# Attention on one core: blocks of three half steps (four heads by 256 queries) with signals of their own, loop written out

## The chip, the cores and the metric

The kernel runs on one core of one Trainium2 chip. The metric is the device time of one execution in microseconds (us); shorter is better.

## The reference, cut to what matters

```python
x = L0_attn_x                                  # (4, 2048, 256)
xn = layernorm(x)
xh, xsh = xn[:, :, :128], holt(xn)[:, :, :128] # holt: exponential smoothing over the sequence
# two branches, each: 8 heads of 16
scores = einsum('bshd,bthd->bhst', q, k) / 4
a = softmax(scores); o = einsum('bhst,bthd->bshd', a, v)
x1 = layernorm(xh + o1 @ wo1.T + bo1); x2 = layernorm(xsh + o2 @ wo2.T + bo2)
y = concatenate([x1, x2], -1)
y = layernorm(y + relu(y @ w_ff1.T + b_ff1) @ w_ff2.T + b_ff2)
out = x + y + (relu(xn @ W1 + b1) @ W2 + b2)   # the "second net"
```

What the change touches is the attention: for each of 4 batches, 2 branches and 8 heads, 2048 by 2048 scores, their exponential, and the product with the values.

## The kernel before, in words

Five engines run programs of their own, tied by semaphores. Each batch has a prologue (normalise, transpose, projections, smoothing, a bound on the maximum), the attention, and the nets that finish the batch. `batches` (L232) runs the prologue of batch 0, then a hardware loop (`Fori`) of three rounds over `middle` (attention of b, prologue of b + 1, nets of b), then `last` written out. Inside the loop, values that a wait compares with depend on b and are computed in registers; in `last` they are constants.

The attention of a batch is 16 units (2 branches, 2 groups of four heads, 4 chunks of 512 queries). A unit runs over 16 key tiles (kt) of 128 keys, so 32 half steps (`STEPS`), and before the change a half step is two heads by 512 queries. On TensorE (PE), in program order (`attention`, L1142):

- scores (L1157): four matmuls per kt, 50 rows by 128 columns, 512 columns moving. The two heads of a half step use the two halves of the array's rows and run side by side. A half step fills one of three PSUM slots of 1024 columns; it waits for the exponential three half steps before.
- one part of the second net (`second_hidden` or `second_out_part`, L994 through `narrow`): 24 matmuls of 256 columns in four column groups, at the eight kts of `NET_KTS` (`FIRST_NET_KTS` in the first unit of a batch); the output projection of the unit before at kt 8, 32 records in the trace.
- values (L1183): four matmuls per kt in four column groups, f32, two records each in the trace, added up in `o_bank`. They wait for both exponentials of the kt and, at kt 0, until DVE has read `o_bank` (`evict`, L679).

The order is scores of kt + 1, then the net's part or the projection, then values of kt. Each of these groups is named S, N or V below. ScalarE (ACT, L585) takes each slot through the exponential into one of four buffers of `p_sb`. DVE evicts and divides a unit's result, takes the bias and relu of the net's hidden part (`hidden_half`, L722), and is still finishing the previous batch (`finish`, L746 to L769) when an attention starts. `second_hidden` waits, from its second part on, until DVE has read the part before (`hid2_read`). POOL and SP issue the DMAs; POOL also adds biases and refills `k_st` and `q_st` when a group's values are done.

## Time and profile before

| | |
|---|---|
| median of 3 runs | 2676.5 us (2676.16 to 2676.57) |
| the profiled execution | 2678.51 us, span 2677.0 us, mean granted clock 0.98 |
| PE busy | 94% of the span |
| ACT busy | 82% |
| DVE busy | 57% |
| POOL busy | 13% |

PE is TensorE's matmuls, PEld its weight loads, ACT ScalarE, DVE VectorE, POOL GpSimd. A row of the timeline merges equal instructions that follow without idle time; the end of a matmul is modelled, so the distance between starts says more than the length. In brackets stands the idle time before, and what ended it.

### The profile page before, as it was taken

How to read it: one execution, taken by the hardware profiler on the slowest of the kernel's cores; microseconds unless marked ns; L12 is line 12 of the kernel's file. 1: busy time of each engine (PE TensorE's matmuls, PEld its weight loads, DVE VectorE, ACT ScalarE, POOL GpSimd, SP SyncE). 2: the span in 40 equal slices, each digit the busy share in tenths (PEclk: the TensorE clock that was granted, in tenths of full speed). 3: DMA queues.
4: the chain of work that ended last, by engine and by line, in shares of the span. 5: the costliest groups of instructions: out<-in, count | busy, mean ns of one | idle time of the engine just before them, and what ended most of it. 6: DMA issues, size and time to landing. Idle time of an engine off the chain costs nothing.

```text
span 2677.0 us, 75084 instructions
## 1 busy us (share of the span) xinstructions
PE 2529.1 (94%) x30049; PEld 1004.4 (38%) x30049; DVE 1516.9 (57%) x3228; ACT 2190.8 (82%) x2411; POOL 355.2 (13%) x349
## 2 busy tenths in 40 slices
PE   5799999999999999998999999999999999999976
PEld 3233333335633333333663333333464333333344
DVE  5344555565764555556575455555567545555576
ACT  3699999994479999997449999999556999999933
POOL 0201010003410100000440101000144010100142
PEclk9899999999999999999999999999999999999988
DMA  4602010003120202000411102000041010100001
GB/s 159 122 10 34 10 34 10 10 10 104 50 65 10 34 14 38 10 6 12 115 49 57 30 14 34 10 10 6 21 122 48 10 34 10 34 10 10 6 25 45
DMA packets 50612, 96.38 MB, mean 36 GB/s; under 512 B 8768, under 2 KB 33344, under 8 KB 49872
## 3 DMA queue, kind: packets, MB, share of 16 engines
q1 hardware_dynamic: 41808, 71.99, 8.9%
q0 software_dynamic: 8448, 19.41, 4.4%
q8 instruction: 251, 4.11, 0.6%
q14 instruction: 105, 0.86, 0.1%
HBM read 57.23 MB, written 34.08 MB: 34 GB/s over the span
## 4 chain that ended last, share of the span: by engine, by line
PE 80%; DVE 7%; issue 5%; POOL 4%; ACT 1%; DMA 1%; SPq 0%; DVEq 0%; POOLq 0%; ACTq 0%
PE slot L1183 34%; PE slot L1157 20%; PE slot L994 16%; POOL p_sb L495 3%; PE slot L1227 2%; PE slot L1079 2%; PE slot L1215 2%; PE slot L1109 1%; DVE o_sb L679 1%; PE slot L1118 1%; PE slot L1107 1%; DVE hid_one L722 1%; DMA k_st<-part_dram 1%; PE slot L1060 1%; ACT p_sb L585 1%
## 5 line engine op out<-in xcount | busy, mean ns | idle before, releaser
L585 ACT ACTIVATE p_sb<-slot 128x1024 f32<-128x1024 f32 x2048 | 1915.7, 1029 | 125.1 <-PE slot L1157 122.4
L1183 PE MATMUL slot<-p_sb,v_sb 128*17 128x512 f32 x8192 | 1071.4, 597 | 23.2 <-DVE o_sb L679 12.6
L1157 PE MATMUL slot<-q_st,k_st 50*128 50x512 f16 x4096 | 624.5, 384 | 23.4 <-DMA k_st<-part_dram 15.4
L1157 PEld LDWEIGHTS slot<-q_st,k_st 50*128 50x128 f16 x4096 | 126.8, 94 | 896.4 <-ACT p_sb L585 715.8
L722 DVE TENSOR_SCALAR hid_one<-slot,b_grown 128x256 f32<-128x256 f32 x256 | 123.8, 484 | 298.9 <-PE slot L994 289.0
L1183 PEld LDWEIGHTS slot<-p_sb,v_sb 128*17 128x17 f32 x8192 | 180.2, 97 | 241.4 <-ACT p_sb L585 211.5
L734 DVE SCALAR_TENSOR_TENSOR second<-slot,second 128x256 f32<-128x256 f32 x64 | 27.2, 425 | 371.1 <-PE slot L994 371.1
L688 DVE RECIPROCAL rden<-den 128x256 f32<-128x256 f32 x128 | 224.4, 1753 | 7.5
L994 PE MATMUL slot<-xt_parts,w_parts 128*32 128x256 f16 x6144 | 214.8, 274 | 1.6 <-DVE hid_one L722 1.6
L994 PE MATMUL slot<-w_parts,hid_parts 128*32 128x256 f16 x6144 | 214.7, 274 | 0.0
L1227 PE MATMUL slot<-wf_parts,p_sb 128*128 128x256 f16 x1536 | 178.0, 275 | 8.7 <-POOL p_sb L495 8.6
L1215 PE MATMUL slot<-area,wf_parts 128*128 128x512 f16 x768 | 173.0, 385 | 12.0 <-DVE area L749 7.2
L994 PEld LDWEIGHTS slot<-xt_parts,w_parts 128*32 128x32 f16 x6144 | 141.0, 96 | 107.7 <-issue 103.0
L994 PEld LDWEIGHTS slot<-w_parts,hid_parts 128*32 128x32 f16 x6144 | 141.2, 96 | 106.6 <-issue 104.6
L486 POOL TENSOR_TENSOR resid<-resid,con 128x1024 f32<-128x1024 f32 x16 | 37.7, 2356 | 1053.7 <-DVEq L744 1053.7
L495 POOL TENSOR_TENSOR p_sb<-area,p_sb 128x512 f16<-128x512 f32 x128 | 148.0, 1157 | 135.7 <-ACT p_sb L601 125.9
L1227 PEld LDWEIGHTS slot<-wf_parts,p_sb 128*128 128x128 f16 x1536 | 149.7, 99 | 36.1 <-POOL p_sb L495 14.7
L368 POOL DMA_DIRECT2D k_st<-part_dram x48 | 24.2, 511 | 954.4 <-PE slot L1183 954.2
L716 DVE TENSOR_TENSOR resid<-slot,resid 128x512 f32<-128x512 f32 x64 | 44.2, 691 | 181.9 <-PE slot L994 181.9
L600 ACT ACTIVATE area<-slot,bf_grown 128x512 f32<-128x512 f32 x128 | 88.0, 687 | 66.2 <-PE slot L1215 39.9
L726 DVE TENSOR_TENSOR hid_parts<-hid_one,hid_parts 128x256 f16<-128x256 f32 x256 | 109.0, 426 | 9.1 <-DVE hid_parts L724 0.5
L1215 PEld LDWEIGHTS slot<-area,wf_parts 128*128 128x128 f16 x768 | 74.8, 99 | 103.9 <-issue 11.2
(101 smaller groups left out, 1833.0 us busy)
## 6 DMA issues: line engine op xcount, KB each, us to landing
part_dram<-p_sb SPq DMA_DIRECT2D x16, 1024.0 KB, 4.0
q_st<-part_dram POOLq DMA_DIRECT2D x96, 128.0 KB, 7.9
xn<-x SPq DMA_DIRECT2D x16, 512.0 KB, 7.6
second<-x SPq DMA_DIRECT2D x32, 256.0 KB, 3.9
ffn_dram<-second SPq DMA_DIRECT2D x32, 256.0 KB, 2.0
area<-ffn_dram SPq DMA_DIRECT2D x16, 512.0 KB, 4.8
out<-area SPq DMA_DIRECT2D x16, 512.0 KB, 3.2
k_st<-part_dram SPq DMA_DIRECT2D x48, 128.0 KB, 12.3
```

What stands on the lines that cost most here:

```text
L495: pool.tensor_tensor(h_lo[:, m, :], h_one[:, m % 2, :], h_hi[:, m, :], ALU.subtract).then_inc(hid_ready, 1)
L585: act.activation(p_sb[:, n % 4, :], slot[n % 3][:, :], ACT.Exp, scale=0.25 / GROW ** 2).then_inc(exp_done, 1)
L600: act.activation(h_one[:, m % 2, :], bank, ACT.Relu, bias=bf_grown[:, m:m + 1])
L688: step(dve.reciprocal(rden[:, cols], den[:, cols]))
L722: dve.tensor_scalar(hid_one[:, :], bank, b1_grown[:, k:k + 1], 0.0, ALU.add, ALU.max).then_inc(hid2_read, 1)
L726: dve.tensor_tensor(hid_lo[:, k, :], hid_one[:, :], hid_hi[:, k, :], ALU.subtract).then_inc(hid2_ready, 1)
L994: mm = pe.matmul(out[ROW * r:ROW * (r + 1), :], lhs[:, ROW * r:ROW * (r + 1)], rhs, start=start, stop=stop, skip_group_check=True)
L1079: mm = pe.matmul(slot[(first + i) % 4][:, k * CHUNK:(k + 1) * CHUNK], wqk[:, 2 * a + which, :], xt[a][:, (2 * i + k) * CHUNK:(2 * i + k + ...
L1157: mm = pe.matmul(slot[at % 3][:, k * CHUNK:(k + 1) * CHUNK], k_st[rows_, pair, kt * P:(kt + 1) * P], q_st[rows_, pair, c_ * CHUNK:(c_ + 1) ...
L1183: mm = pe.matmul(o_bank[ROW * j:ROW * j + DK + 1, :], v_sb[:, a, kt, GH * g + j, :], p_sb[:, n % 4, (j % 2) * CHUNK:(j % 2 + 1) * CHUNK], ...
L1215: mm = pe.matmul(slot[m // 2 % 2][:, (m % 2) * CHUNK:(m % 2 + 1) * CHUNK], w[:, k, m * P:(m + 1) * P], src[:, k * CHUNK:(k + 1) * CHUNK], ...
L1227: mm = pe.matmul(bank[:, t * D:(t + 1) * D], src[:, m, t * P:(t + 1) * P], w[:, m, :], start=(m == 0 and r == 0), stop=(m == HB - 1 and r ...
```

## The change

A half step becomes four heads by 256 queries of one kt (an even half step takes the first half of the chunk, an odd one the second). The 32 half steps of a unit are put into blocks of three (ten of three and one of two). On PE the order is: the scores of a block, each half step into its own of three slots; then the values of the previous block; then a part of the second net or the projection. Each half step has its own exponential, its own signal of scores, of exponential and of values. `p` has six buffers, the third of each block lying in `area`. All hardware loops over batches become Python loops, on all engines. PSUM is one tensor, cut into slots.

```diff
+BLOCKS = [(3 * i, min(3 * i + 3, STEPS)) for i in range(-(-STEPS // 3))]
+LAST_BLOCK = len(BLOCKS) - 1
+HALF_CHUNK = CHUNK // 2
-NET_KTS, FIRST_NET_KTS, PROJECTION_KT = [0, 2, 4, 6, 10, 12, 14, 15], [6, 8, 10, 11, 12, 13, 14, 15], 8
+NET_BLOCKS, FIRST_NET_BLOCKS, PROJECTION_BLOCK = [0, 1, 3, 4, 6, 8, 9, 10], [3, 4, 5, 6, 7, 8, 9, 10], 5
...
+        def batches_in_line(eng, prologue, middle, last):
+
+            prologue(0)
+            for b in range(B - 1):
+                middle(b)
+            last(B - 1)
...
+            p_flat = p_sb[:, :, :].rearrange("p i n -> p (i n)")
+            p_first = p_flat[:, 0:2 * SLOT], p_flat[:, 2 * SLOT:4 * SLOT]
+            p_third = area[:, 3 * SLOT:4 * SLOT], area[:, 0:SLOT]
...
-                    for n in range(UNITS2 * STEPS):
-                        act.wait_ge(scores_made, UNITS2 * STEPS * b + n + 1)
-                        if n % 2 == 0:
-
-                            act.wait_ge(pv_done, UNITS2 * TILES * b + n // 2 + 1)
-                        act.activation(p_sb[:, n % 4, :], slot[n % 3][:, :], ACT.Exp, scale=0.25 / GROW ** 2).then_inc(exp_done, 1)
+                    for unit in range(UNITS2):
+                        u = UNITS2 * b + unit
+                        for i, (lo, hi) in enumerate(BLOCKS):
+                            block = len(BLOCKS) * unit + i
+                            for n in range(lo, hi):
+                                act.wait_ge(scores_made, STEPS * u + n + 1)
+                                if n == lo and block >= 2:
+
+                                    done = BLOCKS[i - 2][1] + (0 if i >= 2 else -STEPS)
+                                    act.wait_ge(pv_done, STEPS * u + done)
+                                p = p_third[block % 2] if n == lo + 2 else p_first[block % 2][:, (n - lo) * SLOT:(n - lo + 1) * SLOT]
+                                act.activation(p, slot[n - lo][:, :], ACT.Exp, scale=0.25 / GROW ** 2).then_inc(exp_done, 1)
...
-                    flat = area[:, 0:2 * FF]
+                    dve.wait_ge(stored, 16 * (CHUNKS * (B - 1) + 1))
+                    flat = area[:, SLOT:SLOT + 2 * FF]
...
-                with step.over(B - 1, PER_MIDDLE) as b:
+                for b in range(B - 1):
                     middle(b)
...
+                        lo, hi = BLOCKS[i]
+                        for n in range(lo, hi):
+
+                            before = n - 3 if i > 0 else (n - 2 if n < 2 else n - 5)
+                            if STEPS * u + before >= 0:
+                                pe.wait_ge(exp_done, STEPS * u + before + 1)
+                            if n == 2 and unit == 0:
                                 pe.wait_ge(ff_read, CHUNKS * b + 1)
+                            kt, tok = n // 2, c_ * CHUNK + n % 2 * HALF_CHUNK
+                            for j in range(GH):
+                                pair, rows_ = GH // 2 * g + j // 2, slice(HALF * (j % 2), HALF * (j % 2) + ROWS)
+                                at = SLOT * (n - lo) + CHUNK * (j % 2) + HALF_CHUNK * (j // 2)
+                                mm = pe.matmul(banks[:, at:at + HALF_CHUNK], k_st[rows_, pair, kt * P:(kt + 1) * P],
+                                               q_st[rows_, pair, tok:tok + HALF_CHUNK], start=True, stop=True)
                             mm.then_inc(scores_made, 1)
...
+                        if i == 0:
+
+                            pe.wait_ge(o_read, u + 1)
+                            if unit == 0:
+                                pe.wait_ge(ff_read, CHUNKS * b + 2)
+                        for n in range(lo, hi):
+                            pe.wait_ge(exp_done, STEPS * u + n + 1)
+                            kt, cols = n // 2, slice(n % 2 * HALF_CHUNK, (n % 2 + 1) * HALF_CHUNK)
+                            p = (p_first if n < lo + 2 else p_third)[block % 2]
+                            for j in range(GH):
+                                at = SLOT * ((n - lo) % 2) + CHUNK * (j % 2) + HALF_CHUNK * (j // 2)
+                                mm = pe.matmul(o_bank[ROW * j:ROW * j + DK + 1, cols], v_sb[:, a, kt, GH * g + j, :], p[:, at:at + HALF_CHUNK],
+                                               start=(n == 0), stop=(n >= STEPS - 2), skip_group_check=True)
+                            mm.then_inc(pv_done, 1)
+
+                    for unit in range(UNITS2):
+                        net_blocks = FIRST_NET_BLOCKS if unit == 0 else NET_BLOCKS
+                        for i in range(len(BLOCKS)):
+
+                            scores(unit, i)
+                            if i > 0:
+                                values(unit, i - 1)
+                            elif unit > 0:
+                                values(unit - 1, LAST_BLOCK)
+                            if i in net_blocks:
+                                (second_out_part if unit % 2 else second_hidden)(b, unit // 2, net_blocks.index(i))
+                            if i == PROJECTION_BLOCK and unit > 0:
                                 out_projection(b, unit - 1)
+                    values(UNITS2 - 1, LAST_BLOCK)
```

## Rows read from the trace of the kernel before

**Rows 1.** The page's chain that ended last: shares by engine, and by line.
```profile
PE 80%; DVE 7%; issue 5%; POOL 4%; ACT 1%; DMA 1%; SPq 0%; DVEq 0%; POOLq 0%; ACTq 0%
PE slot L1183 34%; PE slot L1157 20%; PE slot L994 16%; POOL p_sb L495 3%; PE slot L1227 2%; PE slot L1079 2%; PE slot L1215 2%; PE slot L1109 1%; DVE o_sb L679 1%; PE slot L1118 1%; PE slot L1107 1%; DVE hid_one L722 1%; DMA k_st<-part_dram 1%; PE slot L1060 1%; ACT p_sb L585 1%
```

**Rows 2.** Windows, exponentials (L585) alone, four stretches: us, ACT busy (count), PEclk.
```profile
95.90:594.80 498.90, 479.39 (x512) 0.99 0.11 23
750.50:1248.40 497.90, 479.31 (x512) 0.99 0.10 22
...
2049.70:2543.20 493.50, 477.59 (x512) 1.00 0.08 17
sum 1988.60, ACT 1915.71; mean ACT 478.93
```

**Rows 3.** Timeline, PE, last batch: start, us, engine, line, operation, out<-in, count.
```profile
2176.42 0.60 PE L1157 MATMUL slot<-q_st,k_st 50*128 50x512 f16 x4
2176.95 0.84 PE L994 MATMUL slot<-xt_parts,w_parts 128*32 128x256 f16 x24
2177.62 1.03 PE L1183 MATMUL slot<-p_sb,v_sb 128*17 128x512 f32 x8
2178.59 0.61 PE L1157 MATMUL slot<-q_st,k_st 50*128 50x512 f16 x4
2179.12 1.05 PE L1183 MATMUL slot<-p_sb,v_sb 128*17 128x512 f32 x8
2180.11 0.61 PE L1157 MATMUL slot<-q_st,k_st 50*128 50x512 f16 x4
```

**Rows 4.** Timeline, PE, last batch: a projection and the values behind it.
```profile
2191.77 1.08 PE L994 MATMUL slot<-con,att 128*32 128x128 f32 x32
2192.67 1.04 PE L1183 MATMUL slot<-p_sb,v_sb 128*17 128x512 f32 x8
```

**Rows 5.** Timeline, ACT, last batch, over a unit.
```profile
2163.59 13.03 ACT L585 ACTIVATE p_sb<-slot 128x1024 f32<-128x1024 f32 x14 [0.19 <-PE slot L1157]
...
2179.02 14.87 ACT L585 ACTIVATE p_sb<-slot 128x1024 f32<-128x1024 f32 x16 [0.23 <-PE slot L1157]
2194.07 2.85 ACT L585 ACTIVATE p_sb<-slot 128x1024 f32<-128x1024 f32 x3 [0.19 <-PE slot L1157]
```

**Rows 6.** Timeline, last batch, unit boundary: the eviction on DVE, and values on PE.
```profile
2146.33 0.74 DVE L679 STREAM_SHUFFLE o_sb<-slot 128x512 f32<-128x512 f32 x1
...
2147.12 1.05 PE L1183 MATMUL slot<-p_sb,v_sb 128*17 128x512 f32 x8 [0.24 <-DVE o_sb L679]
```

**Rows 7.** Timeline, first batch (in the loop): scores, and the exponential that waits for them.
```profile
257.63 0.60 PE L1157 MATMUL slot<-q_st,k_st 50*128 50x512 f16 x4
258.14 1.02 ACT L585 ACTIVATE p_sb<-slot 128x1024 f32<-128x1024 f32 x1 [0.53 <-PE slot L1157]
```

**Rows 8.** The chain that ended last, in order of time: start, us, what.
```profile
738.38 8.36 PE slot L1227 x75
```

**Rows 9.** Timeline, PE, end of batch 0's attention: values, then a net's part.
```profile
593.14 1.03 PE L1183 MATMUL slot<-p_sb,v_sb 128*17 128x512 f32 x8
594.00 0.83 PE L994 MATMUL slot<-w_parts,hid_parts 128*32 128x256 f16 x24
```

**Rows 10.** Timeline, last batch, first unit: DVE, PE, and the next unit's start on ACT.
```profile
2054.06 6.78 DVE L635 TENSOR_SCALAR rs<-mv 128x4 f32<-128x4 f32 x1
...
2067.18 0.48 DVE L722 TENSOR_SCALAR hid_one<-slot,b_grown 128x256 f32<-128x256 f32 x1 [0.21 <-DVE area L768]
...
2067.72 0.84 PE L994 MATMUL slot<-xt_parts,w_parts 128*32 128x256 f16 x24 [1.55 <-DVE hid_one L722]
...
2082.12 1.94 ACT L585 ACTIVATE p_sb<-slot 128x1024 f32<-128x1024 f32 x2 [0.23 <-PE slot L1157]
```

**Rows 11.** Timeline, PE: first scores behind a loop's end, and behind the last round.
```profile
749.86 0.23 PEld L1157 LDWEIGHTS slot<-q_st,k_st 50*128 50x128 f16 x4 [3.40 <-issue]
...
2049.30 0.82 PE L1157 MATMUL slot<-q_st,k_st 50*128 50x512 f16 x6
```

More of the change, by code:

```diff
@@ L212, in rows @@
             return con[:, lo:hi].rearrange("p (k n) -> p k n", k=1).broadcast_to([P, k, hi - lo])
-        slot = [ctx.enter_context(nc.psum_tensor(f"slot{i}", [P, SLOT], f32)) for i in range(4)]
+        banks = ctx.enter_context(nc.psum_tensor("banks", [P, 4 * SLOT], f32))
+        slot = [banks[:, i * SLOT:(i + 1) * SLOT] for i in range(4)]
         def sem(name):
@@ L434, in last @@
                     attention(b, False)
-                    hold(sp, pv_done, TILES * UNITS2 * (b + 1) + 2)
+                    hold(sp, pv_done, STEPS * UNITS2 * (b + 1))
                     results(b)
@@ L449, in sync_program @@
                         sp.dma_start(k_st[at:at + 2, pair, :], k_ones).then_inc(ones_out, 16)
-                batches(sp, prologue, middle, last)
+                batches_in_line(sp, prologue, middle, last)
                 sp.wait_ge(second_out, 16 * (HALVES * B + 2))
@@ L527, in pool_program @@
                 pool.wait_ge(ones_out, 16 * HEADS)
-                batches(pool, first, middle, last)
+                batches_in_line(pool, first, middle, last)
             def scalar_program(act):
@@ L625, in scalar_program @@
                 act.wait_ge(consts_in, 16)
-                batches(act, first, middle, last)
+                batches_in_line(act, first, middle, last)
             def vector_program(dve):
@@ L677, in evict @@
                     u = UNITS2 * b + n
-                    hold(dve, pv_done, TILES * (u + 1) + 2)
+                    hold(dve, pv_done, STEPS * (u + 1))
                     dve.stream_shuffle(o_sb[:, :], o_bank, O_ROWS).then_inc(o_read, 1)
@@ L793, in turn @@
                         src = slot[place % 4][:, 0:P]
-                        if a == 1 or not isinstance(b, int):
+                        if 2 * b + a > 0:
                             dve.wait_ge(m_out, 16 * (2 * b + a))
@@ L1142, in attention, with scores @@
                 def attention(b):
-                    def scores(unit, kt):
+                    def scores(unit, i):
                         a, g, c_ = UNIT_LIST[unit]
-                        if kt == 0 and c_ == 0:
+                        u = UNITS2 * b + unit
+                        if i == 0 and c_ == 0:
                             hold(pe, stack_in[g], 16 * ((K_LOADS + 2 * Q_LOADS) * b + (Q_LOADS, K_LOADS + 2 * Q_LOADS)[a]))
@@ L1148, in scores @@
                                 hold(pe, k_first_in[g], 16 * K_LOADS * (b + 1))
-                        for n in (2 * kt, 2 * kt + 1):
-                            at = STEPS * unit + n
-                            pe.wait_ge(exp_done, UNITS2 * STEPS * b + at - 2 + 3)
-                            if at == 2:
-                                pe.wait_ge(ff_read, CHUNKS * b + 1)
-                            for k in range(2):
-                                pair, rows_ = GH // 2 * g + n % 2, slice(HALF * k, HALF * k + ROWS)
-                                mm = pe.matmul(slot[at % 3][:, k * CHUNK:(k + 1) * CHUNK], k_st[rows_, pair, kt * P:(kt + 1) * P],
-                                               q_st[rows_, pair, c_ * CHUNK:(c_ + 1) * CHUNK], start=True, stop=True)
+                        lo, hi = BLOCKS[i]
@@ L1159, in scores, with values @@
                             mm.then_inc(scores_made, 1)
-                    scores(0, 0)
-                    for unit, (a, g, c_) in enumerate(UNIT_LIST):
+                    def values(unit, i):
+                        a, g, c_ = UNIT_LIST[unit]
                         u = UNITS2 * b + unit
-                        net_kts = FIRST_NET_KTS if unit == 0 else NET_KTS
-                        for kt in range(TILES):
-                            if kt + 1 < TILES:
-                                scores(unit, kt + 1)
-                            elif unit + 1 < UNITS2:
-                                scores(unit + 1, 0)
-                            if kt in net_kts:
-                                (second_out_part if unit % 2 else second_hidden)(b, unit // 2, net_kts.index(kt))
-                            if kt == PROJECTION_KT and unit > 0:
-                                out_projection(b, unit - 1)
-                            if kt == 0:
-                                pe.wait_ge(o_read, u + 1)
-                                if unit == 0:
-                                    pe.wait_ge(ff_read, CHUNKS * b + 2)
-                            pe.wait_ge(exp_done, STEPS * u + 2 * kt + 2 + 3)
-                            for j in range(GH):
-                                n = 2 * kt + j // 2
-                                mm = pe.matmul(o_bank[ROW * j:ROW * j + DK + 1, :], v_sb[:, a, kt, GH * g + j, :],
-                                               p_sb[:, n % 4, (j % 2) * CHUNK:(j % 2 + 1) * CHUNK],
-                                               start=(kt == 0), stop=(kt == TILES - 1), skip_group_check=True)
-                            mm.then_inc(pv_done, 1)
@@ new lines, in values @@
+                        lo, hi = BLOCKS[i]
+                        block = len(BLOCKS) * unit + i
+                        if i == 0:
[11 more added lines that the diff above has]
+                            mm.then_inc(pv_done, 1)
@@ L1250, in last @@
                     nets(b)
-                pe.sem_inc(pv_done, 2)
                 pe.sem_inc(net_done, 1)
                 pe.wait_ge(consts_in, 16)
-                batches(pe, first, middle, last)
+                batches_in_line(pe, first, middle, last)
                 pe.wait_ge(added, 2)
```

4 lines of the change are left out of this document (1 added, 3 removed).

## The prediction

> **What bounds the kernel now.** I read the page first: the chain that ended last is 80% PE, and over half of it is two lines, values (L1183) and scores (L1157) [rows 1]. The windows on L585 come next: the 2048 exponentials fill four stretches, 1988.6 us of the 2677.0 us, one per batch with 16 units each [rows 2]. So a unit is about 31 us, and there are 64.
>
> The order of time on PE shows what a unit is made of [rows 3]. I call S the scores of one kt, V its values, N one part of the second net. S to the next group takes 0.53 us, N 0.67, V up to the following S 0.99 after an S and 0.97 after an N. A kt without N is 1.52 us, one with N 2.17. Sixteen kts, eight Ns and one projection of 0.90 [rows 4] make 16 x 1.52 + 8 x 0.65 + 0.90 = 30.4 us on PE. ACT needs 2.85 us for three exponentials [rows 5] and 1.02 for one [rows 7], so 0.917 each in a stream, 29.3 us a unit. A unit of the last batch lasts 30.48 us (2163.59 to 2194.07 [rows 5]), the mean of a batch inside the loop is 497.9 / 16, about 31.0 [rows 2]. So **PE's in-order stream is the bound, and ACT is only 1.1 us a unit behind it**. What exceeds 30.4 is, in every second unit, V waiting for the DVE eviction at a boundary (0.24 us of PE idle, some 0.4 in all [rows 6]); and, inside the loop, ACT starting 0.51 us after its scores (257.63 to 258.14 [rows 7]) where the written-out last batch has 0.43 (2178.59 to 2179.02 [rows 3, 5]).
>
> **The change, part by part.**
>
> *Cost of the pieces.* Scores: before, two rounds of 512 columns take 0.53 with about 0.10 of changeover, 0.215 a round. After, a half step is two rounds of 256 columns, each with its own weights. Lower bound 0.215; upper from the second linear layer of the net, 75 matmuls of 256 columns with their own weights in 8.36 us [rows 8], 0.111 a round, 0.223. I take 0.220. Values: V takes about 0.86 of its 0.99, so half the columns take 0.431. The leading 0.014 after an S stays. Changeovers: S to V or N 0.10, V to S 0.11. V to N costs nothing: 593.14 to 594.00 is 0.86 for a whole V [rows 9]. **N to S does not occur in the trace** (N is always followed by V today), and the change makes it the rule, 8 times a unit. Bounds: 0, as N to V, and 0.11, as V to S. I take 0.11, since N like V is a four-column-group form and S a two-row-group form, and each change between these two kinds that the trace shows costs 0.10 or 0.11.
> The Trainium skill ("TensorEngine Tiling (Array Packing)", Key Properties) says that a change of tiling mode, not merely of tile, drains the engine. The trace agrees for S to V and V to S, and by that rule N to S is a drain too.
>
> *A block on PE.* Three score half steps 0.66 + 0.11, three value half steps 1.31, N 0.655, changeover 0.11: 2.84 us. ACT's three exponentials: 2.75. Without N a block is 2.18, with the projection 3.08. PE saves five pairs of changeovers a unit (11 instead of 16, about 1.1 us), adds a little for more rounds, and would need about 29 us, under ACT's 29.3. If the two overlapped freely this would be a gain of 1 to 1.5 us a unit.
>
> *The new wait.* They don't overlap freely. Slot 2 is freed by the last exponential of the previous block, and the third S of a block waits for it. Behind that wait in PE's queue stand all values of the previous block, N or the projection, and the first scores of the next block; ACT has then just three exponentials left. From the end of that exponential to the end of the first of the block after: signal about 0.05 (my estimate, no row times it alone), S 0.22 + 0.10, V 1.31, N 0.655, changeover 0.11, scores to exponential 0.43 [rows 3, 5], exponential 1.02 [rows 7]: 3.90 us. ACT could have been there after 4 x 0.917 = 3.67. So **a block with N that follows a loose one stalls ACT 0.23**; one that follows a tight block stalls by PE's own excess, 0.09; the projection block 0.33. The short block is the worst: between the scores of block 10 and those of the next unit stand two S, three V and N, 2 x 0.22 + 0.11 + 1.31 + 0.655 + 0.11 = 2.62, and they are covered by two exponentials, 1.83: a stall of 0.79. Iteration 0 has only two V and is loose again. N stands in blocks 0, 1, 3, 4, 6, 8, 9, 10, the projection in 5: stalls after block 1, 3 and 8 of 0.23 each, 4, 6 and 9 of 0.09 each, 5 of 0.33, 10 of 0.79, in all 2.08. **A unit: 29.33 + 2.08 = 31.4 us**, against a mean of 31.0 (loop) or 30.7 (last batch) now. In this the boundary wait for DVE is gone: V of the next unit comes after N and three S, 1.5 us or more behind the last V, and the eviction takes 0.74 [rows 6].
>
> *First unit of batches 1 to 3.* N parts start at block 3, the second at block 4, about 13 us into the batch. But DVE is still finishing the previous batch, with one step of 6.78 us, and it reads the first part only at 2067.18, 17.9 us after the first scores (2049.30). Already now PE waits 1.55 us there, at kt 8, and the unit lasts 32.4 (first exponential 0.43 after 2049.30, next unit's 2082.12) [rows 10, 11]. After, it waits at block 4, with 12 value half steps done instead of 16. From 18.4 us: N and changeover 0.76, five blocks of 2.84, 2.62 for the last, so 36.0 us for the unit. Batch 0 has no such wait, yet its stretch is 1.0 us longer than that of batch 1 [rows 2]: some 2 us of slow start, which stay, on 31.0 for a first unit without the wait (eight blocks with N, no short block ahead), 32.9.
>
> *Sum of attention, first exponential's start to last one's end.* The last unit counts to its last end, 31.4 - 0.79 - 0.92 + 1.02 = 30.7. Batch 0: 32.9 + 14 x 31.4 + 30.7 = 503.2. Batches 1 to 3: 36.0 + 439.6 + 30.7 = 506.3 each. Together 2022.1 against 1988.6 [rows 2]: **+33.5 us**.
>
> *Loop written out.* After the last net matmul PE idles 3.40 us where the loop closes; after the last iteration the first scores follow at 2049.30 with no such idle [rows 11]. Two such places, about 3.2 each: -6.4. In the prologues inside the loop the waits lose their register work too. The trace has no row for one hop of them but ACT's, 0.51 against 0.43 [rows 3, 5, 7]; with some ten such hops in series that is about 1 us a prologue (0 to 2): -3. The nets stay: PE streams there. The shorter ACT delay (0.43) is in the units above.
>
> *End of attention.* The last V after the last exponential is one half step, 0.43, not a whole V, 0.86: about -0.5 x 4 = -2. SP, POOL: same DMAs, the same points of release (pv_done counts half steps; the last V of a unit still releases the stacks). The third buffer lies in memory that only prologue and results use; last batch's weight tests now wait for stores finished long before. Nothing for these.
>
> **Sum:** 33.5 - 6.4 - 3 - 2 = +22 us. The profiled execution took 2678.5 us with a span of 2677.0, 2 us over the median 2676.5, so I add the difference to the median: 2699, **+0.8%**.
>
> **The rivals.**
>
> *Faster: the changeover from N to S is hidden.* Then every net block loses 0.11, the stalls of 0.09 vanish, those of 0.23 become 0.12, the short block 0.68; a unit is about 30.75, and 60 ordinary units give 60 x 0.65 = 39 us back: 2660. The sign turns at a changeover of about 0.05. For it: N to V and V to N are free. Against: both keep the form of the groups, N to S doesn't. 0.17.
>
> *Scores of 256 columns do not pair.* If the second pair of a half step can't load its weights under the first, a round grows by a load, and at the worst the four matmuls of a half step run one by one: 4 x 0.107 = 0.43 instead of 0.22. PE would then bound every block, 0.64 more in each: some 5 us a unit, near 3000. Against: N's loads, same length, hide at 256 columns (24 matmuls in 0.67 us, four side by side [rows 3]).
> The Trainium skill ("TensorE: Matmul & The Clock Gate", The mechanism) says a weight load overlaps running matmuls only when the row group differs, which is this rival's result; N's rows speak against it, since all its groups use the same rows. 0.05.
>
> *PE's instruction supply.* A unit holds 1216 weight loads and matmuls instead of 832, 39 a us instead of 27. The densest long stretch now is a run of kts with N, 72 in 2.17 us, 33 a us; for 0.67 us N alone runs at 72. If 33 were a limit a unit would be 36.8, again near 3000. 0.03.
>
> *No change within 0.2%* (about what a measurement of this kernel can tell from none: 2671 to 2682): DVE's wait in the first units smaller, a changeover of 0.05 to 0.07. 0.09.
>
> *Forecast* 2682 to 2722: 0.66. Chances: faster 0.17, same 0.09, slower 0.74. The range reaches to the faster rival and, above, to rounds of 0.24 or values at 0.44 (0.2 to 0.3 a unit): 2657 to 2725.
>
> **What would show it.** A second unit in mid-batch of 31.4 us, ACT idle about 0.7 to 0.8 once a unit behind scores of the first block; idles near 0.2 after net blocks; N's last round to the next S about 0.2 us; no wait on DVE o_sb; a PE wait of some 5 us on hid_one in batches 1 to 3; PE's 3.4 us idle at the two loop ends gone; ACT 0.43 after its scores everywhere. Wrong if a unit is under 31.0 (then N to S or the short block is mis-sized) or over 32.

## The result and the profile after

The changed kernel took 2720.1 us (median of 4 runs, 2716.8 to 2721.8) against 2676.5: a ratio of 1.0161, interval 1.0143 to 1.0178. It is slower, by 43.6 us. The profiled execution took 2716.8 us, with a span of 2715.2. Every ratio below is to the kernel before, measured again beside each experiment (medians 2678.5, 2677.6 and 2677.5). Two single executions, one of the kernel before and one of halves_only, took 4160 and 4158 us at a mean granted clock of 0.56 and are left out of every comparison.

The page of after: the engines, the queue that brings instructions, and the chain that ended last, by engine and by line.

```profile
PE 2499.7 (92%) x42337; PEld 1486.3 (55%) x42337; DVE 1516.0 (56%) x3228; ACT 2202.2 (81%) x2411; POOL 353.9 (13%) x349
...
q8 instruction: 334, 5.47, 0.8%
...
PE 68%; ACT 20%; DVE 6%; issue 2%; DMA 2%; POOL 2%; SPq 0%; DVEq 0%; ACTq 0%; POOLq 0%
PE banks L1201 27%; PE banks L1181 14%; PE banks L1013 13%; ACT p_sb L604 12%; ACT area L604 6%; PE banks L1259 5%; PE banks L1247 4%; PE banks L1098 2%; PE banks L1128 1%; POOL p_sb L508 1%; DVE rs L653 1%; DMA part_dram<-p_sb 1%; PE banks L1126 1%; ACT p_sb L620 1%; ACT area L619 1%
```

ACT had 1% of the chain before [rows 1] and has 20% now: the chain passes from PE to ACT and back in every unit, which is what a handshake looks like that neither engine wins. PE is 29 us less busy than before (2499.7 against 2529.1) and the span is 38 us longer.

The exponentials' windows, answering to [rows 2]: us, ACT busy (count), PEclk, DMA share, GB/s.

```profile
95.83:600.03 504.20, 482.09 (x512) 0.99 0.10 23
749.54:1259.93 510.39, 482.01 (x512) 0.99 0.09 22
1408.74:1919.10 510.36, 482.01 (x512) 0.99 0.10 22
2067.70:2578.07 510.37, 482.01 (x512) 0.99 0.08 18
sum 2035.32, ACT 1928.12; mean ACT 482.03
```

Attention grew by 46.7 us (forecast 33.5). Between the stretches lie 446.9 us, against 458.7 in [rows 2]: 11.8 us less. After the last exponential come 137.1 us against 133.8. That adds up to the 38.2 us of the spans; the medians differ by 5 more, since before's profiled execution was 2.0 us above its median and after's 3.3 below. Single runs scatter by more than that: after's by 5 us, and before's, 30 single runs in all, from 2675.0 to 2686.5.

One ordinary unit of the last batch, ACT. The starts give the length of every block (the ends are modelled):

```profile
2135.28 1.94 ACT L604 ACTIVATE p_sb<-banks 128x1024 f32<-128x1024 f32 x2
2137.90 1.94 ACT L604 ACTIVATE p_sb<-banks 128x1024 f32<-128x1024 f32 x2 [0.68 <-PE banks L1181]
...
2140.63 1.96 ACT L604 ACTIVATE p_sb<-banks 128x1024 f32<-128x1024 f32 x2
...
2143.65 1.94 ACT L604 ACTIVATE p_sb<-banks 128x1024 f32<-128x1024 f32 x2
...
2152.23 1.94 ACT L604 ACTIVATE p_sb<-banks 128x1024 f32<-128x1024 f32 x2
...
2155.35 1.94 ACT L604 ACTIVATE p_sb<-banks 128x1024 f32<-128x1024 f32 x2 [0.27 <-PE banks L1181]
...
2169.39 1.94 ACT L604 ACTIVATE p_sb<-banks 128x1024 f32<-128x1024 f32 x2 [0.68 <-PE banks L1181]
```

A unit is 2169.39 - 2137.90 = 31.49 us; the forecast was 31.4. The two exponentials of the short block take 2137.90 - 2135.28 = 2.62 us instead of 1.83: a stall of 0.79, exactly the forecast one. Block 1 takes 3.02 (2140.63 to 2143.65), a stall of 0.27 over 2.75; forecast 0.23. Block 5, with the projection, takes 2155.35 - 2152.23 = 3.12, 0.37; forecast 0.33. All eleven blocks of this unit, from the starts of the same view, the left-out ones too: 2.73, 3.02, 2.72, 3.02, 2.84, 3.12, 2.84, 2.73, 3.01, 2.84, 2.62.

PE over blocks with a net part, the same unit:

```profile
2146.56 0.39 PE L1181 MATMUL banks<-q_st,k_st 50*128 50x256 f16 x4 [0.52 <-ACT area L604]
2146.88 1.06 PE L1201 MATMUL banks<-p_sb,v_sb 128*17 128x256 f32 x16
2147.75 0.61 PE L1201 MATMUL banks<-area,v_sb 128*17 128x256 f32 x8
2148.18 0.84 PE L1013 MATMUL banks<-xt_parts,w_parts 128*32 128x256 f16 x24
2148.96 0.83 PE L1181 MATMUL banks<-q_st,k_st 50*128 50x256 f16 x12
2149.72 1.06 PE L1201 MATMUL banks<-p_sb,v_sb 128*17 128x256 f32 x16
```

From values to values it is 2149.72 - 2146.88 = 2.84 us, the forecast block. Three scores with their changeover take 0.76 (forecast 3 x 0.22 + 0.10), two value half steps 0.87, the third 0.43. **N to S is 0.78, where N to V was 0.67 [rows 3]: the unknown changeover is 0.11.** The [0.52] ahead of the third scores is the wait for slot 2, the new wait.

### The profile page after: what moved, and what is told of

It reads as the page before. It is cut to its first block, busy times and chain, and to the rows that moved or that the text cites. A ratio compares the mean times of both kernels' runs of the same rounds, so it can differ in the third digit from the quotient of the medians.

```text
span 2715.2 us, 93007 instructions
## 1 busy us (share of the span) xinstructions
PE 2499.7 (92%) x42337; PEld 1486.3 (55%) x42337; DVE 1516.0 (56%) x3228; ACT 2202.2 (81%) x2411; POOL 353.9 (13%) x349
## 3 DMA queue, kind: packets, MB, share of 16 engines
q8 instruction: 334, 5.47, 0.8%
## 4 chain that ended last, share of the span: by engine, by line
PE 68%; ACT 20%; DVE 6%; issue 2%; DMA 2%; POOL 2%; SPq 0%; DVEq 0%; ACTq 0%; POOLq 0%
PE banks L1201 27%; PE banks L1181 14%; PE banks L1013 13%; ACT p_sb L604 12%; ACT area L604 6%; PE banks L1259 5%; PE banks L1247 4%; PE banks L1098 2%; PE banks L1128 1%; POOL p_sb L508 1%; DVE rs L653 1%; DMA part_dram<-p_sb 1%; PE banks L1126 1%; ACT p_sb L620 1%; ACT area L619 1%
## 5 line engine op out<-in xcount | busy, mean ns | idle before, releaser
L604 ACT ACTIVATE p_sb<-banks 128x1024 f32<-128x1024 f32 x1408 | 1369.3, 1029 | 152.7 <-PE banks L1181 126.8
L1201 PE MATMUL banks<-p_sb,v_sb 128*17 128x256 f32 x11264 | 751.1, 385 | 0.0
L1181 PE MATMUL banks<-q_st,k_st 50*128 50x256 f16 x8192 | 618.6, 273 | 103.0 <-ACT area L604 83.4
L604 ACT ACTIVATE area<-banks 128x1024 f32<-128x1024 f32 x640 | 668.0, 1044 | 0.0
L1181 PEld LDWEIGHTS banks<-q_st,k_st 50*128 50x128 f16 x8192 | 309.4, 94 | 392.6 <-issue 162.6
L1201 PEld LDWEIGHTS banks<-p_sb,v_sb 128*17 128x17 f32 x11264 | 260.0, 97 | 290.2 <-issue 137.7
L1201 PE MATMUL banks<-area,v_sb 128*17 128x256 f32 x5120 | 396.2, 382 | 0.0
L1013 PE MATMUL banks<-xt_parts,w_parts 128*32 128x256 f16 x6144 | 217.0, 275 | 11.4 <-DVE hid_one L740 11.4
L1013 PE MATMUL banks<-w_parts,hid_parts 128*32 128x256 f16 x6144 | 214.5, 273 | 0.0
L1259 PE MATMUL banks<-wf_parts,p_sb 128*128 128x256 f16 x1536 | 175.9, 273 | 7.9 <-POOL p_sb L508 7.9
L1259 PEld LDWEIGHTS banks<-wf_parts,p_sb 128*128 128x128 f16 x1536 | 149.0, 98 | 33.9 <-POOL p_sb L508 13.2
```

The costliest lines, as they stand in the source:

```text
L604: act.activation(p, slot[n - lo][:, :], ACT.Exp, scale=0.25 / GROW ** 2).then_inc(exp_done, 1)
L1013: mm = pe.matmul(out[ROW * r:ROW * (r + 1), :], lhs[:, ROW * r:ROW * (r + 1)], rhs, start=start, stop=stop, skip_group_check=True)
L1181: mm = pe.matmul(banks[:, at:at + HALF_CHUNK], k_st[rows_, pair, kt * P:(kt + 1) * P], q_st[rows_, pair, tok:tok + HALF_CHUNK], start=True ...
L1201: mm = pe.matmul(o_bank[ROW * j:ROW * j + DK + 1, cols], v_sb[:, a, kt, GH * g + j, :], p[:, at:at + HALF_CHUNK], start=(n == 0), stop=(n ...
L1259: mm = pe.matmul(bank[:, t * D:(t + 1) * D], src[:, m, t * P:(t + 1) * P], w[:, m, :], start=(m == 0 and r == 0), stop=(m == HB - 1 and r ...
```

## The experiments

### The loop alone

```diff
 # kernel before, all five programs and DVE's own loop
-                batches(pe, first, middle, last)
+                batches_in_line(pe, first, middle, last)
...
-                with step.over(B - 1, PER_MIDDLE) as b:
+                for b in range(B - 1):
                     middle(b)
```

> The kernel before with its hardware loops over batches written out and nothing else. My theory (the new blocks cost, the written-out loop gives back): a unit in batches 0 to 2 falls from a mean of 31.0 to the last batch's 30.7, 48 x 0.31 = 15 us, the two loop ends give 6.4, the prologues 3: 2652 us. Rival (writing the loop out is itself a cost, for instance by instruction supply): 2677 or more, units at 31.0 or above.

Measured, loop_only: 2656.8 us (2656.1 to 2660.6), ratio 0.9918, interval 0.9901 to 0.9935; forecast 2652. PE at the first loop end, and ACT in batch 0:

```profile
729.20 8.36 PE L1234 MATMUL slot<-wf_parts,p_sb 128*128 128x256 f16 x75 [0.32 <-POOL p_sb L502]
737.50 0.82 PE L1164 MATMUL slot<-q_st,k_st 50*128 50x512 f16 x6
```
```profile
209.17 13.04 ACT L592 ACTIVATE p_sb<-slot 128x1024 f32<-128x1024 f32 x14 [0.19 <-PE slot L1164]
...
224.60 14.87 ACT L592 ACTIVATE p_sb<-slot 128x1024 f32<-128x1024 f32 x16 [0.23 <-PE slot L1164]
239.65 13.04 ACT L592 ACTIVATE p_sb<-slot 128x1024 f32<-128x1024 f32 x14 [0.19 <-PE slot L1164]
...
255.52 14.87 ACT L592 ACTIVATE p_sb<-slot 128x1024 f32<-128x1024 f32 x16 [0.66 <-PE slot L1164]
```

The 3.40 us of [rows 11] are gone. Units alternate between 30.48 (209.17 to 239.65) and 30.92 (224.60 to 255.52), and all four stretches last 493.0 to 493.7 us, what only the written-out batch did before [rows 2]. So writing the loop out gains about 20 us by itself, 15 of it in attention, and the rest of the change costs more than the 43.6 us that were measured: about 63.

### Half steps of four heads by 256 queries, in the old order

```diff
 # loop_only, scores
-                            for k in range(2):
-                                pair, rows_ = GH // 2 * g + n % 2, slice(HALF * k, HALF * k + ROWS)
...
+                            for j in range(GH):
+                                pair, rows_ = GH // 2 * g + j // 2, slice(HALF * (j % 2), HALF * (j % 2) + ROWS)
+                                col = CHUNK * (j % 2) + CHUNK // 2 * (j // 2)
...
 # values: a half step at a time, each with its wait
+                            for n in (2 * kt, 2 * kt + 1):
+                                pe.wait_ge(exp_done, STEPS * u + n + 1 + 3)
```

> loop_only with the half step of four heads by 256 queries, each half step of the values waiting for its own exponential; the order per kt (scores of the next, net, values), the three slots and the four buffers stay as before, no blocks of three. My theory (it is the grouping in blocks of three that costs, not the smaller matmuls): within 0.4 us a unit of loop_only, so 2652 to 2672. Rival (256-column matmuls with twice the weight loads and signals cost the time): a unit of 31.5 or more, 2700 or above.

Measured, halves_only: 2664.8 us, ratio 0.9939, interval 0.9918 to 0.9960; 8 us more than loop_only. The units are 30.96 and 30.53, 0.04 above loop_only's. So 256 columns pair as well as 512, PE takes 39 instructions a us, and two of the rivals (some 3000 us) fall. Most of the rest, 6.8 us, is in one or two longer units of every batch, the fifth and the ninth, by up to 1.8 us, where POOL refills `k_st` and `q_st`. In the last batch PE stops some 12 us behind the start of the refill (2157.16). PE there, and the window around it (us, busy time of PE, PEld, DVE, ACT and POOL, PEclk, DMA share, GB/s):

```profile
2168.78 0.61 PE L1194 MATMUL slot<-p_sb,v_sb 128*17 128x256 f32 x8
2170.44 0.63 PE L1194 MATMUL slot<-p_sb,v_sb 128*17 128x256 f32 x8 [1.06 <-ACT p_sb L592]
```
```profile
2167.00:2171.00 4.00, 2.94 (x60) 1.33 (x53) 2.18 (x5) 3.25 (x4) 0.00 (x0) 1.00 1.03 131
```

ACT is named as the releaser, but ACT itself idles here (3.25 us busy in a window of 4.00), so the cause is another. The DMA engines are busy throughout this window (share 1.03), and in the trace the instruction queue's 16 KB packets, which came every 6 to 7 us up to here, come at 2156.16 and then only at 2167.13. That PE had run out of fetched code fits these rows and was not tested by itself.

### The net's last part moved from block 10 to block 7

```diff
-NET_BLOCKS, FIRST_NET_BLOCKS, PROJECTION_BLOCK = [0, 1, 3, 4, 6, 8, 9, 10],
+NET_BLOCKS, FIRST_NET_BLOCKS, PROJECTION_BLOCK = [0, 1, 3, 4, 6, 7, 8, 9],
```

> The changed kernel with one part of the second net moved from block 10, before the short cover of two exponentials, to block 7. My theory: at the unit's boundary PE then has 1.96 us between the last scores of a unit and the first of the next, and the stall there falls from 0.79 to about 0.13, with 0.06 more beside it; a unit of 30.85 instead of 31.49, 60 x 0.64 = 38 us off: 2682 us. Rival (the boundary stall comes from the eviction on DVE or from the signals there): the 0.79 stays, 2720.

Measured, net_10_to_7: 2685.7 us (10 runs, 2681.8 to 2686.3), ratio 1.0021, interval 1.0010 to 1.0032: 34 us less than after (forecast 38), for one net part moved. ACT over a unit:

```profile
2144.68 3.90 ACT L604 ACTIVATE p_sb<-banks 128x1024 f32<-128x1024 f32 x4
...
2175.58 3.90 ACT L604 ACTIVATE p_sb<-banks 128x1024 f32<-128x1024 f32 x4
```

A unit is 30.90 us (forecast 30.85), and the boundary has no idle time worth a bracket. The short block's stall is real: moving the part is worth 0.59 a unit. after's order put a net part behind the one block that has two exponentials to cover it.

### The net's part before the values

```diff
                             scores(unit, i)
+                            if i in net_blocks:
+                                (second_out_part if unit % 2 else second_hidden)(b, unit // 2, net_blocks.index(i))
...
                             if i > 0:
                                 values(unit, i - 1)
```

> The changed kernel with the net's part or the projection between the scores and the values instead of behind the values. The changeovers are as many, but it is V and not N that stands ahead of the scores. Theory (a changeover of 0.10 to 0.11 between four column groups and two row groups, the same for N and V; the path behind the third scores holds the same work): a unit of 31.4 to 31.6 again, 2720. Rival (the change from N to the scores is a cost of the new order): a unit of 30.8, 2680.

Measured, net_before_values: 2729.1 us, ratio 1.0193, interval 1.0176 to 1.0210. PE around a net part:

```profile
2157.04 0.84 PE L1013 MATMUL banks<-xt_parts,w_parts 128*32 128x256 f16 x24
2157.70 1.04 PE L1201 MATMUL banks<-p_sb,v_sb 128*17 128x256 f32 x16
2158.57 0.60 PE L1201 MATMUL banks<-area,v_sb 128*17 128x256 f32 x8
2159.10 0.92 PE L1181 MATMUL banks<-q_st,k_st 50*128 50x256 f16 x12
```

N takes 0.66 now, but the values' last piece takes 0.53 (2158.57 to 2159.10) instead of 0.43: the changeover has moved from N to V, at 0.10. Half of the units are 31.43 us, as forecast. The other half are 31.87: with the net one values' group earlier, its part also asks earlier for what DVE has read, which the waits show.

```profile
PE banks L1013 <- DVE hid_one L740: 26.2, 31, 5.3
```

In after it is 3 waits, 11.4 us. The price by the changeover is settled; that order is worse for a reason that was not in the expectation.

### Less of the net

```diff
                         for n, (src, w) in enumerate(((hid_hi, w2_hi), (hid_hi, w2_lo), (hid_lo, w2_hi))):
-                            mm = narrow(side[:, t * D:(t + 1) * D], src[:, m, t * P:(t + 1) * P], w[:, m, :], ...
 # and so in the hidden part
```

> The changed kernel with the second net's parts cut from six rounds of matmuls to one (two terms of three, and most of the sum, are left out, so its output is not the reference's); all signals stay. Theory (the stalls come from PE work behind the third scores of a block): ACT streams, with one stall of some 0.4 at the projection, a unit of 29.8, near 2620. Rival (the waits and signals of each half step, or six buffers, stall ACT by themselves): stalls of 0.2 stay in many blocks, a unit above 30.5.

Measured, thin_net: 2609.2 us, in a single run. ACT over a unit:

```profile
2129.92 1.94 ACT L604 ACTIVATE p_sb<-banks 128x1024 f32<-128x1024 f32 x2 [0.36 <-PE banks L1182]
...
2159.72 1.94 ACT L604 ACTIVATE p_sb<-banks 128x1024 f32<-128x1024 f32 x2 [0.36 <-PE banks L1182]
```

A unit is 29.80, as forecast: 32 exponentials at 0.917 are 29.34, and the one stall that is left belongs to the projection's block. With little net behind the slot's wait the structure does reach ACT's rate. So it is not the waits and signals as such that cost. This kernel also has less work on PE in all, so alone it doesn't separate how much PE does from where it stands. net_10_to_7 does: the same work, one part elsewhere in the queue, 0.59 us a unit. The total is 11 us under the forecast since the first units of batches 1 to 3 also shrank, to 35.0 to 35.6.

### POOL's addition later

The 9.94 us addition of a bias on POOL (L485) runs while DVE finishes the previous batch. This kernel holds it back until the last row block of `finish` is through. In after, last batch, the two stand like this:

```profile
2072.47 6.79 DVE L653 TENSOR_SCALAR rs<-mv 128x4 f32<-128x4 f32 x1
```
```profile
2069.28 9.94 POOL L485 TENSOR_TENSOR resid<-xn,con 128x4096 f32<-128x4096 f32 x1 [10.37 <-DVE area L776]
```

```diff
                     pool.wait_ge(ff_read, CHUNKS * b + 2)
+                    pool.wait_ge(o_ready, CHUNKS * b + 1)
                     pool.tensor_tensor(resid[:, :, :], xn[:, :, :], rows("bo", TILES), ALU.add).then_inc(xn_used, 1)
```

> The changed kernel, POOL's 9.94 us residual addition of the next batch held back until DVE has finished the previous batch. Theory: DVE's step of over 6 us in the first unit is a wait for POOL's operation; without it DVE reads the first net part some 6.6 us sooner, PE waits no longer at block 4, the clock stays at 1.0 there, and the first unit of batches 1 to 3 falls from 38.7 to 31.5 to 32.5: 19 to 21 us off, 2700 us. Rival (the step is long by itself): 2720, unchanged. If only the wait goes and the low clock stays, the first unit is about 34.

Measured, pool_late: 2720.7 us, ratio 1.0153, interval 1.0136 to 1.0170: no change against after. The forecast gain of some 20 us did not come, and DVE, POOL and PE tell why.

```profile
2081.32 7.23 DVE L743 CAST hid_parts<-hid_one 128x256 f16<-128x256 f32 x1
```
```profile
2079.49 8.91 POOL L486 TENSOR_TENSOR resid<-xn,con 128x4096 f32<-128x4096 f32 x1 [19.64 <-DVE area L787]
```
```profile
2089.70 1.47 PE L1014 MATMUL banks<-xt_parts,w_parts 128*32 128x256 f16 x24 [3.92 <-DVE hid_one L741]
```

The step of 6.8 us in `finish` is gone, but a cast that takes 0.29 elsewhere takes 7.23 now, and both end where POOL's addition ends (in after 2079.26 and 2079.22, here 2088.55 and 2088.40). PE waits 3.92 us one block later. **The long DVE step was never DVE's: it is one DVE instruction held until POOL's long one is over**, and moving POOL's moved the victim. POOL's own took 8.91 us here and 9.94 in after, where a DVE addition with two inputs in SBUF had started just ahead of it.

The Trainium skill ("SBUF — State Buffer", Who interferes with whom) has this rule: the two engines share a pair of ports as a lock for a whole instruction, which on DVE's side a cast or a tensor-scalar can want, and the one that comes second waits. Trace and rule agree, and I had read the 6.78 us of [rows 10] as given, where the rule would have led to POOL.

### POOL's addition in eight pieces

```diff
-                    pool.tensor_tensor(resid[:, :, :], xn[:, :, :], rows("bo", TILES), ALU.add).then_inc(xn_used, 1)
+                    for k in range(HB):
+                        pool.wait_ge(hid2_ready, HB * HALVES * b + k + 1)
+                        part = slice(2 * k, 2 * k + 2)
+                        pool.tensor_tensor(resid[:, part, :], xn[:, part, :], rows("bo", 2), ALU.add).then_inc(resid_part, 1)
```

> The changed kernel with POOL's residual addition cut into eight pieces of two tiles, each released when DVE has finished one part of the first unit's hidden layer, when DVE waits for PE anyway. Theory (POOL's long operation holds DVE wherever it stands, the wait then stops PE for 4 us and the granted clock falls to 0.5 behind it): no PE wait on hid_one over 0.5 us, clock 1.0 from 2080 on, the first unit of batches 1 to 3 is 32 to 33 instead of 38.7, 2700 us. Rival (the first unit is long by its blocks of nets alone): 37 or more, 2715.

Measured, pool_spread: 2698.7 us (2698.2 to 2705.2), ratio 1.0077, interval 1.0060 to 1.0094: 21 us less than after. POOL and the same DVE step, last batch, and the first unit's two ends on ACT:

```profile
2076.53 1.28 POOL L489 TENSOR_TENSOR resid<-xn,con 128x512 f32<-128x512 f32 x1 [21.20 <-DVE hid_parts L750]
```
```profile
2068.44 0.17 DVE L659 TENSOR_SCALAR rs<-mv 128x4 f32<-128x4 f32 x1
```
```profile
2064.11 1.94 ACT L610 ACTIVATE p_sb<-banks 128x1024 f32<-128x1024 f32 x2 [10.02 <-PE banks L1187]
...
2095.21 1.94 ACT L610 ACTIVATE p_sb<-banks 128x1024 f32<-128x1024 f32 x2 [0.68 <-PE banks L1187]
```

0.17 us where it was 6.79, and a first unit of 31.10 instead of 38.71. Batches 1 to 3 have 32.0, 31.1 and 31.1: 7.3 us less each on average, 22 in all, which fits the 21 us between the medians. (32.0 is the one of the three in which the clock fell just behind the start of the batch.)

The profiled execution itself shows only 11.5 of them (span 2703.7 against 2715.2). It was 6 us above the other three, and two things take the difference to after back. Four units behind the refills are longer by 0.6 to 1.2 us. And two of the three gaps between attentions are 152.5 us where after has 148.6 to 149.5. There the clock falls: the same 51 matmuls at the end of batch 1 and of batch 0.

```profile
1331.28 7.41 PE L1265 MATMUL banks<-wf_parts,p_sb 128*128 128x256 f16 x51 [0.64 <-POOL p_sb L514]
```
```profile
676.12 5.74 PE L1265 MATMUL banks<-wf_parts,p_sb 128*128 128x256 f16 x51 [0.65 <-POOL p_sb L514]
```

For 3.4 us from 1331.74 on PE was granted 0.50, and at 676.12 it had 1.00. Over the eleven profiled kernels with the loop written out, 9 of 33 gaps have this fall, about 75 us into the gap: they last 151.2 to 152.6 us, the other 24 148.6 to 150.2. Profiled were single executions, and kernels that differ only in the attention (kt_spread and kt_first) have it in different gaps, so I take these 2 us each for scatter and not for an effect of a change; that is not tested.

### The best block order, and the best old order

Blocks, with both cures (and the pieces of POOL as above):

```diff
-NET_BLOCKS, FIRST_NET_BLOCKS, PROJECTION_BLOCK = [0, 1, 3, 4, 6, 8, 9, 10],
+NET_BLOCKS, FIRST_NET_BLOCKS, PROJECTION_BLOCK = [0, 2, 3, 4, 6, 7, 8, 9],
```

> The changed kernel with the net parts in blocks 0, 2, 3, 4, 6, 7, 8, 9, so that none stands in the short block and two loose blocks stand near the boundary, and POOL's addition in eight pieces. Theory (the stalls add up as in the prediction): a unit of 30.71 to 30.76, first units of 31 to 32, 2720 - 45 - 20 = 2655 to 2658 us, level with loop_only: blocks of three can be repaired, not made to win. Rival (another limit of the blocks appears below 31): 2670 or more.

Measured, blocks_best: 2657.3 us (2654.4 to 2662.9), ratio 0.9912, interval 0.9886 to 0.9938. Units are 30.74, with one or two in each batch longer by 0.5 to 1.5 us, behind the refills as in halves_only.

The old order in loop_only, with POOL in pieces, and the net's last two parts moved off the boundary:

```diff
-NET_KTS, FIRST_NET_KTS, PROJECTION_KT = [0, 2, 4, 6, 10, 12, 14, 15], ...
+NET_KTS, FIRST_NET_KTS, PROJECTION_KT = [0, 2, 4, 6, 10, 12, 13, 14], ...
```

> loop_only (the old order per kt, loop written out) with the last net part of a unit at kt 13, 14 instead of 14, 15, and POOL's residual addition in eight pieces as in pool_spread. Theory: the wait for the eviction at every second unit's boundary goes, 30.92 becomes 30.48, 13 us off; the first units lose the 1.6 us wait for DVE, 5 us off: 2639 us, faster than both kernels. Rival (the boundary is bound by something else): 2652 or more.

Measured, kt_spread: 2639.8 us, ratio 0.9863, interval 0.9846 to 0.9879. From the third unit of a batch on all but three are 30.48 or 30.49. Every unit had a net part at kt 15, just ahead of the boundary, but only a hidden part leaves DVE its relu to do: in before DVE works on it until 2146.04 and starts the eviction at 2146.33 [rows 6]. It is the units behind those that were 30.92.

And with the first unit's parts earlier, [5, 7, 8, 9, 10, 12, 13, 14]:

> kt_spread with the first unit's net parts at kt 5, 7, 8, 9, 10, 12, 13, 14, so that the second unit's boundary no longer waits for the eviction. Theory: the second unit of each batch falls from 31.57 to about 30.5, 4 us in all, 2636 us. Rival (DVE, still finishing the previous batch, then stops PE at kt 7): first units above 31.5 and no gain, 2640 or more.

Measured, kt_first: 2638.3 us (2638.0 to 2639.4), ratio 0.9845, interval 0.9821 to 0.9869. ACT over a unit of the last batch, and the windows of the last batch and of all four together:

```profile
2104.32 18.59 ACT L598 ACTIVATE p_sb<-slot 128x1024 f32<-128x1024 f32 x20 [0.23 <-PE slot L1170]
...
2134.81 18.59 ACT L598 ACTIVATE p_sb<-slot 128x1024 f32<-128x1024 f32 x20 [0.23 <-PE slot L1170]
```
```profile
...
2012.26:2500.36 488.10, 478.05 (x512) 1.00 0.09 18
sum 1953.62, ACT 1912.33; mean ACT 478.08
```

The four second units did fall from 31.57 to 30.48 us, and the attention of all batches from 1958.0 to 1953.6, the forecast 4 us, though the first units of batches 1 to 3 grew from 30.8 to 31.1. Of this the medians show 1.5 us (2636 was forecast), which the intervals can't tell from none; in the profiled execution one gap has the clock's fall of pool_spread.

kt_first and kt_spread are the fastest, 37 to 38 us under before, and they have neither blocks of three nor the new half steps. With POOL's addition in pieces in both, the best blocks (blocks_best) stay some 18 us behind them. A unit of kt_first (2104.32 to 2134.81) is 30.49 us, and the bound is again PE's own 30.4.

## Why the prediction was right in sign and short in size

The forecast was +22 us, 2699, within 2682 to 2722; measured were +43.6 and 2720.1. The sign came from the mechanism that was forecast. That the time still lies in the range, near its upper end, is in part luck: the range was made for longer rounds and values, and what filled it was something else. Against the sum, attention gave 13.2 us more, the stretches between 0.9 less, the end of the program 3.8 more, and the medians 5.3 more than the profiled executions.

**The unit.** Forecast 31.4, measured 31.49. The stalls, forecast against measured (block length less 2.75, for the short one less 1.83): after blocks with net behind loose ones 0.23 against 0.27, 0.27 and 0.26; tight ones 0.09 against 0.09 three times; the projection 0.33 against 0.37; the short block 0.79 against 0.79. Against these 0.03 to 0.04, the three loose blocks are 0.02 to 0.03 under 2.75, so a unit is some 0.08 over the sum, and 60 units 5 us. The signal, an estimate of 0.05, has a row now: the third exponential of a block ends at 2146.50 (2145.47 and 1.03 long), and the third scores behind it start at 2146.56. net_10_to_7 and thin_net, each forecast to 0.05 us a unit from the same chain, show that the reasoning was right. One aside of the prediction is off: its own pieces make 29.5 us of PE for a unit (ten blocks of 2.18, a short one of 1.53, eight Ns, the projection), not "about 29", so PE was never under ACT's 29.3. No term of the sum rests on it.

**N to S.** Taken as 0.11 between bounds of 0 and 0.11, measured as 0.11, and net_before_values shows it stays (0.10) when it is moved. The rule of the Trainium skill ("TensorEngine Tiling (Array Packing)", Key Properties) that a change of tiling mode drains the engine holds here: S to V, V to S, and N to S cost 0.10 to 0.11, N to V and V to N nothing. This was the faster rival's condition, and it fell.

**The two rivals near 3000.** Both fell in halves_only. The weight loads of the second pair of scores are hidden though both pairs use the same rows (two pairs 0.22 us), as [rows 3] had shown for N. That goes against the sentence of the Trainium skill ("TensorE: Matmul & The Clock Gate", The mechanism) by which they overlap only where the row group differs.

**The first units of batches 1 to 3: this step failed in size.** Forecast 36.0, measured 38.79, 38.58 and 38.71, 8 us in all. The place and the wait (DVE not done with the previous batch when the second part of the net asks) were as described. PE in after, first unit of the last batch, and windows with the granted clock (the column behind the five busy times):

```profile
2085.94 1.47 PE L1013 MATMUL banks<-xt_parts,w_parts 128*32 128x256 f16 x24 [4.11 <-DVE hid_one L740]
2087.35 1.46 PE L1181 MATMUL banks<-q_st,k_st 50*128 50x256 f16 x12
2088.74 1.91 PE L1201 MATMUL banks<-p_sb,v_sb 128*17 128x256 f32 x16
```
```profile
2080.00:2086.00 6.00, 1.89 (x36) 0.79 (x36) 5.58 (x16) 2.85 (x3) 0.00 (x0) 0.84 0.00 0
2086.00:2090.00 4.00, 4.00 (x49) 1.95 (x53) 1.84 (x5) 2.00 (x3) 0.00 (x0) 0.50 0.86 266
```

PE comes back 18.67 us after its first scores (2067.27); forecast 18.4. But it comes back at a granted clock of 0.50, which is 1.2 GHz: N takes 1.41 instead of 0.77, the scores 1.39 instead of 0.76, and the values to 2091.11 take 2.37 instead of 1.31. That is 2.33 us of the 2.7. Before, the same wait was 1.55 us [rows 10] and the clock there stayed at 1.00, so the sum had no term for it: **a wait that grows from 1.5 to 4 us costs the time after it too.** pool_spread takes the wait away, the clock there stays at 1.00, and the unit is 31.1.

**Attention, in all.** 13.2 us over the forecast: 8.1 from three first units, 5.4 from four times 14 or 15 other units, less 0.3 in the first unit of batch 0 (32.55 against 32.9).

**The loop ends.** Forecast were -6.4 for two, -3 for the prologues and -2 for the ends of attention. Between the stretches that made -10.9, and it is -11.8; the first gap went from 155.7 us [rows 2] to 149.5. The total fits by luck, its parts less so. The loop ends gave 3.4 each. The prologues gave little: before's third gap, with its prologue inside the loop and no loop end behind it, is 149.9 us, and loop_only's three are 148.8 to 150.2, 149.6 on the mean; 1 us each was forecast. before's first gap has the clock's fall that pool_spread showed (51 matmuls in 7.41 us at 669.98, 5.74 at 1322.61) and after's has none, which is some 2 us of chance.

In every batch both half steps of the last block come behind the last exponential (0.86 us), as the whole values did before, so that end saved nothing. Behind the last stretch -0.5 was forecast and it is +3.3: from DVE's last instruction to the end of the span it is 9.4 us in after and 6.4 before. loop_only has it too (9.5), so it comes with the written-out loop; no row shows what fills it.

**The rest.** The measured medians differ by 5 us more than the profiled spans, which is within what single runs do. Two kinds of scatter can be seen in the profiles: the clock's fall in the gaps, 2 us each, and the longer units behind the refills, where instruction packets come late (5.47 MB of them, against 4.11 before). Which of them made the 5 us here stays open.

## What to carry to other kernels

When a group of work is put behind one wait, count what stands in the queue between that wait and the next signal, and compare it with the work that the other engine still holds: the shortest group decides, and moving one item off it was worth 34 us here (with one more moved, and POOL's addition in pieces, 63). Look at a suspiciously long instruction on one engine together with what runs on the others at that time, and cut the long one into pieces that run while the other engine waits, rather than shift it whole. Do the parts of a compound change alone: here writing out the loop gained 20 us, the new half steps lost 8 (most of it behind the refills, where after loses only 0.3), and the blocks lost some 55 (some 20 of them by POOL's long addition, which PE had waited for less before), so the measured loss hid a gain.

## What the runs showed of the hardware

- A POOL addition of 128 x 4096 f32 (9 to 10 us) held a DVE instruction in SBUF alone until it ended: a tensor-scalar of 128 x 4 took 6.79 us instead of 0.17, a cast of 128 x 256 took 7.23 instead of 0.29. Other DVE instructions ran beside it at their usual lengths (batch-norm statistics 1.41 us, a tensor-scalar that reads PSUM 0.48). In pieces of 128 x 512 (1.3 us) nothing was held, but no cast and no tensor-scalar with all its data in SBUF ran beside a piece either, so whether a piece would hold one was not seen.
- In a wait of 4.11 us (2081.83 to 2085.94) the granted clock fell to 0.50 at 2084.11 and stayed there until 2090.94, so for 5.0 us of PE's work after the wait. After a wait of 1.55 us it was 1.00.
- The clock also fell in some starts of batches 1 to 3 of the kernels with blocks, 3.2 to 4.4 us after the first scores, with 2.0 of the first 3.7 us busy on PE: three times in after, once in pool_spread, never in blocks_best, in 11 of 21 starts over the seven profiled. PE's rows up to there are the same. It never fell in the 12 starts of the four kernels with the old order and the loop written out. Why it falls in one start with blocks and not in the other stays open; in pool_spread the first unit is 32.0 us where it falls and 31.1 where it doesn't.
- Four loads and matmuls of 50 rows x 128 and 256 columns take 0.22 us in pairs. PE ran 39 instructions a us over a unit without waiting for them, but for the places behind the refills, where late instruction packets fit the rows and were not tested.
- A fall of the clock to 0.50 for 3.4 us in a dense stretch of PE work made 51 matmuls of 128 x 256 last 7.41 us instead of 5.74.
- A hardware loop's end over a batch cost 3.4 us of idle PE; waits on register values inside it cost ACT 0.08 a hop (0.51 against 0.43).
